# A decoder layer on one core: the prologue of the pair pipeline in another order

## What is computed

```python
def layer(x, c):                                # (32, 64, 256) each
    q, k, v = split(x @ w_project.T)            # 16 heads of 16
    a = softmax(causal(q @ k.T / 4)) @ v
    x = layernorm(x + a @ w_out.T)              # "norm1"
    q, k = rotary(Wq x + bq), rotary(Wk c + bk) # channels on the
    v = Wv c + bv                               #   64 axis, 8 heads of 8
    x = layernorm(x + Wo (softmax(q @ k.T / sqrt(8)) @ v) + bo)
    return layernorm(x + ffn(x))                # two quantised linears
```

## Time and profile before

| | us |
|---|---|
| median of 3 runs | 615.06 (614.21 to 616.49) |
| the profiled execution | 616.69 |
| its span, first to last instruction | 614.5 |
| busy: PE, DVE, ACT, POOL | 477.7, 461.1, 393.7, 301.7 |
| mean granted TensorE clock | 0.814 of full speed |

### The profile page before, as it was taken

One profiled execution on the slowest core, in us unless ns is written; L12 is line 12 of the kernel. 1 busy time (PEld: TensorE's weight loads), 2 busy tenths in 40 slices (PEclk: granted clock), 3 DMA queues, 4 the chain that ended last, 5 costly groups with the idle time before them and its releaser, 6 DMA issues. The chain is left out here.

```text
span 614.5 us, 12481 instructions
## 1 busy us (share of the span) xinstructions
PE 477.7 (78%) x4162; PEld 259.5 (42%) x4162; DVE 461.1 (75%) x954; ACT 393.7 (64%) x729; POOL 301.7 (49%) x430
## 2 busy tenths in 40 slices
PE   5457899999999999999999999798665055544455
PEld 3435445555555455555545544333221033333333
DVE  2544787887987987987987988665467678888885
ACT  1212166767766766766866867777589577777763
POOL 3425546547547447457447445000200577777772
PEclk9666699999999999999999999659669555555555
DMA  5115236333233233223223222100000000000001
GB/s 190 43 22 182 70 88 194 97 83 98 57 83 97 59 84 98 62 77 99 68 70 99 72 58 77 39 2 2 0 1 0 0 0 19 18 17 17 17 17 34
DMA packets 51399, 37.04 MB, mean 60 GB/s; under 512 B 21392, under 2 KB 47376, under 8 KB 51216
## 3 DMA queue, kind: packets, MB, share of 16 engines
q1 hardware_dynamic: 51344, 36.33, 20.9%
HBM read 24.52 MB, written 10.49 MB: 57 GB/s over the span
## 5 line engine op out<-in xcount | busy, mean ns | idle before, releaser
L914 DVE TENSOR_REDUCE MX<-mx_b 128x2 f32<-128x512 f32 x256 | 167.8, 678 | 40.0 <-PE mx_b L541 38.8
L730 ACT ACTIVATE PB<-e_b 128x512 f32<-128x512 f32 x256 | 149.6, 593 | 67.8 <-PE e_b L569 66.9
L541 PE MATMUL mx_b<-KA,QA 48*128 48x256 bf16 x512 | 101.1, 285 | 7.6 <-DVE MX L914 7.5
L569 PE MATMUL e_b<-QA,KA 50*128 50x256 bf16 x512 | 101.4, 282 | 2.3 <-ACT PB L730 2.3
L586 PE MATMUL u_b<-PB,VA 128*32 128x256 f32 x1024 | 86.9, 406 | 3.9 <-ACT PB L730 3.4
L841 POOL TENSOR_TENSOR SP<-SP,srec 128x1024 f32<-128x1024 f32 x16 | 30.4, 1902 | 82.7 <-DVE srec L886 82.7
L541 PEld LDWEIGHTS mx_b<-KA,QA 48*128 48x128 bf16 x512 | 30.2, 95 | 86.2 <-issue 48.6
L1329 PE MATMUL r_b<-att_tab,Q 128*128 128x128 f32 x128 | 31.5, 427 | 37.5 <-ACT Q L1253 37.3
L1321 PE MATMUL z_b<-w2q,Q2T 128*128 128x256 bf16 x128 | 30.2, 417 | 37.0 <-ACT Q2T L1276 31.7
L301 POOL TENSOR_TENSOR rs<-mv,epsc 128x1 f32<-128x1 f32 x32 | 6.1, 192 | 89.0 <-DVE mv L288 58.8
L836 POOL TENSOR_TENSOR KM<-QK,att_tab 128x512 f32<-128x512 f32 x32 | 32.6, 1042 | 30.9 <-ACT QK L684 30.9
(11 more groups left out here) (144 smaller groups left out, 1091.7 us busy)
## 6 DMA issues: line engine op xcount, KB each, us to landing
KA<-parts_k SPq DMA_DIRECT2D x64, 96.0 KB
QA<-parts_q SPq DMA_DIRECT2D x64, 96.0 KB
parts_q<-part_q SPq DMA_DIRECT2D x32, 128.0 KB, 1.9
parts_k<-part_k SPq DMA_DIRECT2D x16, 192.0 KB, 2.1
XT<-in_xT SPq DMA_DIRECT2D x16, 128.0 KB, 2.1
C<-in_ctx SPq DMA_DIRECT2D x16, 128.0 KB, 3.0
X<-in_x SPq DMA_DIRECT2D x16, 128.0 KB, 3.0
out_y<-O SPq DMA_DIRECT2D x16, 128.0 KB, 1.7
```

Of the source, the lines that this page charges most:

```text
L541: m = nc.tensor.matmul(mx_b[n % 2][:, D * k:D * k + D], QA[low:low + K_MAX, 2 * i.ring + b, h, P * u:P * u + P], KA[low:low + K_MAX, 2 * i ...
L569: m = nc.tensor.matmul(e_b[n % 2][:, D * k:D * k + D], KA[low:low + K_EXP, 2 * i.ring + b, h, P * sc:P * sc + P], QA[low:low + K_EXP, 2 * ...
L730: nc.scalar.activation(PB[:, n % 4].rearrange("p e t -> p (e t)"), e_b[n % 2][:, :], ACT.Exp, scale=XC ** -0.5).then_inc(e_sb.sem, 1)
L914: nc.vector.tensor_reduce(MX[:, b, e, 2 * q:2 * q + 2, u], mx_b[n % 2][:, :].rearrange("p (e s) -> p e s", e=2), AXL.X, ALU.max).then_inc( ...
```

## The change

The arithmetic stays. What moves:

- The first loads: wp in two pieces (Q and K, then V, with a semaphore of its own), and XT of pair 0 and the tables issued by ScalarE ahead of its work. A one-element Exp stands first on ScalarE, so that its table load comes there.
- TensorE: QK before V; the waits for tables and fills stand only before their first use; rotary projections and V projections of the prologue write to mx_b and e_b; QK, scores and V of pair 2 come into the prologue, QK of pair 2 ahead of pair 1's transposes.
- Masks of pair 0: half c = 0 on VectorE, c = 1 on GpSimd. KA's fills: ring 0 and 2 on GpSimd, ring 1 on VectorE. `self_norm` of pairs 0 and 1 on VectorE.
- VectorE rotates K of pair 0 behind the subtraction; ScalarE makes norm1 of pair 0 ahead of pair 1's exp, and `v_copy` of pair 1 behind it.
- In the bodies the steps of pair 2 that the prologue now holds are left out (`fresh`).

The diff, cut to its core:

```diff
+        def fresh(pair):
+
+            return real(pair) and pair.v > 2
...
                 elif n == "k":
-                    sp.wait_ge(s_pad, 2 * j.ring + 2)
+                    sp.wait_ge(s_pad[j.ring], 2)
                 sp.wait_ge(stored[n][j.p], NSTORE * (j.uses + 1))
                 dst = {"q": QA, "k": KA}[n]
                 for e in range(2):
...
             p0, p1, p2, p3 = (Pair(0, a) for a in range(4))
-            sp.dma_start(wp[:], wpT.rearrange("(k p) n -> p k n", p=P)).then_inc(ld_wp, 16)
-            load_xT(p0)
-            sp.dma_start(att_tab[:], attn_tables).then_inc(ld_att, 16)
+            wpk = wpT.rearrange("(k p) n -> p k n", p=P)
+            sp.dma_start(wp[:, :, 0:2 * D], wpk[:, :, 0:2 * D]).then_inc(ld_wp, 16)
+            sp.dma_start(wp[:, :, 2 * D:3 * D], wpk[:, :, 2 * D:3 * D]).then_inc(ld_wv, 16)
             load_c(p0)
...
+            def qk_proj(a, bank):
 
                 pe.wait_ge(ld_xT[a.p], 16 * (a.uses + 1))
-                ps = use(g_b[2], qk_sb, a, 1)
+                ps = use(bank, qk_sb, a, 1)
                 for c in range(4):
                     for k in range(2):
                         last = nc.tensor.matmul(ps[:, P * c:P * c + P], wp[:, k, P * c:P * c + P],
                                                 XT[:, a.p, k, :], start=k == 0, stop=k == 1)
                 last.then_inc(qk_ps.sem, 1)
...
-                    wait(pe, km, a, c + 1)
+                    wait(pe, km[c], a, 1)
                     for r in range(2):
                         for b in range(2):
...
-                pe.wait_ge(s_late, 4)
+                pe.wait_ge(s_late, NLATE)
                 nc.tensor.matmul(g_b[g][:, 0:2], ones[:], wsum[:], start=True, stop=True).then_inc(s_wtot, 1)
 
             pe.wait_ge(ld_wp, 16)
-            pe.wait_ge(s_tab, 2)
-            pe.wait_ge(s_init, NINIT)
 
...
-                        qk_proj(a)
+                    if s == 1 and fresh(a):
+                        qk_proj(a, g_b[2])
                     if s == 2 and real(i):
...
             def prologue():
                 p0, p1, p2 = (Pair(0, n) for n in range(3))
-                v_proj(p0)
-                qk_proj(p0)
-                rotary_proj("k", g_b[2], p0)
+                qk_proj(p0, g_b[2])
+                pe.wait_ge(ld_wv, 16)
+                v_proj(p0, mx_b[0])
+                rotary_proj("k", e_b[0], p0)
+                pe.wait_ge(s_tab, 2)
                 scores(p0)
-                qk_proj(p1)
+                qk_proj(p1, g_b[2])
+                pe.wait_ge(s_init, NINIT)
                 transpose_p(p0)
                 self_pv(p0)
-                v_proj(p1)
                 out_proj(p0)
                 scores(p1)
-                rotary_proj("q", g_b[2], p0)
-                rotary_proj("k", g_b[2], p1)
+                v_proj(p1, mx_b[0])
+                rotary_proj("q", mx_b[1], p0)
+                rotary_proj("k", e_b[1], p1)
+                qk_proj(p2, g_b[2])
                 transpose_p(p1)
                 self_pv(p1)
                 out_proj(p1)
-                v_proj(p2)
+                scores(p2)
+                v_proj(p2, e_b[0])
...
                                      scale=winv[:, k:k + 1]).then_inc(s_wround, 1)
 
+            act.dma_start(XT[:, 0], xT[0]).then_inc(ld_xT[0], 16)
+            act.dma_start(att_tab[:], attn_tables).then_inc(ld_att, 16)
             act.wait_ge(s_init, NINIT)
+
+            nc.scalar.activation(warm[:], half[:], ACT.Exp)
 
             def prologue():
                 p0, p1, p2 = (Pair(0, n) for n in range(3))
-                v_copy(p0)
-                qk_copy(p0)
+                qk_copy(p0, g_b[2])
+                v_copy(p0, mx_b[0])
                 self_exp(p0, 1)
                 self_exp(p0, 0)
-                qk_copy(p1)
+                qk_copy(p1, g_b[2])
                 pt_copy(p0)
                 ao_copy(p0)
-                v_copy(p1)
+                norm1(p0)
                 self_exp(p1, 1)
                 self_exp(p1, 0)
-                norm1(p0)
+                v_copy(p1, mx_b[0])
+                qk_copy(p2, g_b[2])
                 pt_copy(p1)
                 ao_copy(p1)
-                v_copy(p2)
+                v_copy(p2, e_b[0])
+                self_exp(p2, 1)
+                self_exp(p2, 0)
 
...
-        def k_mask(pool, a):
-
-            wait(pool, qk_sb, a, 1)
-            for c in range(2):
-                if has(a, 1):
-                    wait(pool, sc_ps, a.plus(-1), 1)
-                nc.gpsimd.tensor_tensor(KM[:, c], QK[:, 2 + c, :].unsqueeze(1).broadcast_to([P, 4, P]),
-                                        kmask.unsqueeze(2).broadcast_to([P, 4, P]), ALU.mult).then_inc(km.sem, 1)
+        def k_mask(eng, ops, a, c, ev):
+
+            wait(eng, qk_sb, a, 1)
+            if has(a, 1):
+                wait(eng, sc_ps, a.plus(-1), 1)
+            ops.tensor_tensor(KM[:, c], QK[:, 2 + c, :].unsqueeze(1).broadcast_to([P, 4, P]),
+                      kmask.unsqueeze(2).broadcast_to([P, 4, P]), ALU.mult).then_inc(ev[c].sem, 1)
+
+        def ones_rows(ops, r):
+            for e in range(2):
+                ops.memset(KA[HALF * e + 32:HALF * e + 64, 2 * r:2 * r + 2].rearrange("p a h t -> p (a h t)"),
+                           1.0).then_inc(s_pad[r], 1)
 
...
             def prologue():
-                p0, p1 = Pair(0, 0), Pair(0, 1)
-                ones_rows(0)
+                p0, p1, p2 = (Pair(0, n) for n in range(3))
+                k_mask(dve, nc.vector, p0, 0, km)
                 row_max(p0, 1)
                 row_max(p0, 0)
-                rotate("k", g_b[2], p0)
                 minus_max(p0, 1)
                 minus_max(p0, 0)
-                ones_rows(1)
+                rotate("k", e_b[0], p0)
                 self_sum(p0)
+                self_norm(dve, nc.vector, p0)
+                ones_rows(nc.vector, 1)
                 norm1_stats(p0)
                 row_max(p1, 1)
                 row_max(p1, 0)
                 minus_max(p1, 1)
                 minus_max(p1, 0)
-                rotate("q", g_b[2], p0)
+                rotate("q", mx_b[1], p0)
                 self_sum(p1)
-                rotate("k", g_b[2], p1)
-                ones_rows(2)
+                self_norm(dve, nc.vector, p1)
+                rotate("k", e_b[1], p1)
                 norm1_stats(p1)
+                row_max(p2, 1)
+                row_max(p2, 0)
+                minus_max(p2, 1)
+                minus_max(p2, 0)
 
...
+            pool.wait_ge(s_ones, 1)
+            pool.wait_ge(s_late, NLATE)
+            pool.wait_ge(s_init, NINIT)
+            ones_rows(nc.gpsimd, 0)
+            pool.wait_ge(s_pad[0], 2)
             pool.wait_ge(ld_att, 16)
-            pool.wait_ge(s_init, NINIT)
 
             def prologue():
-                p0, p1 = Pair(0, 0), Pair(0, 1)
-                k_mask(pool, p0)
+                p0, p1, p2 = (Pair(0, n) for n in range(3))
+                k_mask(pool, nc.gpsimd, p0, 1, km)
                 split_parts(pool, nc.gpsimd, "k", p0)
-                self_norm(pool, nc.gpsimd, p0)
-                k_mask(pool, p1)
+                for c in range(2):
+                    k_mask(pool, nc.gpsimd, p1, c, km)
+                wait(pool, km[1], p1, 1)
+                ones_rows(nc.gpsimd, 2)
+                pool.wait_ge(s_pad[2], 2)
                 rstd(pool, ln1, p0, mv1, rs1)
                 split_parts(pool, nc.gpsimd, "q", p0)
-                self_norm(pool, nc.gpsimd, p1)
+                for c in range(2):
+                    k_mask(pool, nc.gpsimd, p2, c, km)
                 split_parts(pool, nc.gpsimd, "k", p1)
 
```

56 lines of the change are left out of this document (26 added, 30 removed).

## The result

The changed kernel takes **608.5 us** (median of 4 runs, 607.18 to 609.98) against 614.87 for the kernel before, run beside it: a ratio of 0.9893, 95% interval 0.9862 to 0.9925, or 6.4 us. The prediction was 607.1, with a range that takes in 604 and 610, and the measured median lies inside.

The account below looks back on a forecast made before the run. TensorE paces the loop from 79 us; before it a chain of waits bounds the start. First e_b at 70.5 for 78.50, 8.0 us earlier and handed on whole: 615.06 - 8.0 = 607.1 us, range taking in 604 and 610.

Parts of the forecast that it names:

- Start: First loads to the end of pair 0's scores: these end at 12.9 us for 14.80, 1.9 us earlier.
- Pair 0's softmax: Pair 0's scores to transposes: transposes at 19.2 us for 26.20, 7.0 earlier, about 4 from VectorE's two fills.
- VectorE against GpSimd: Rival, chance 0.15: pair 0's normalisation on VectorE waits 0.6 us for GpSimd's split of K; gain 7.4, 607.7 us.
- Pair 1 and the new wait: Pair 1's transposes wait behind QK of pair 2 for its XT: 39.9 us for 48.16, the wait taking back 4.
- First mx_b: First mx_b tile, behind scores and V of pair 2: at 50.6 us for 59.06, 8.5 earlier.
- Body -1: Last piece before the loop: rotary projection waits for norm1 until 53.4 us; first e_b at 70.5 for 78.50, 8.0 earlier.
- the tail: From the V projection of pair 3 to the first e_b in body -1: stays at 6.83 us.
- From there to the end: From the first e_b to the end of the span: the same length as before, 536 us.
- The rival of the high clock: Chance 0.2: the clock rises in body -1 and stays, rotation 0.9 us sooner, tail 1.8 shorter; gain 10.7, 604.4 us.
- The other waits: Rival, chance 0.14: late first load 1.2 us, ScalarE's new order 1, KA's fills on GpSimd 1; gain 5, 610.1 us.
- no effect: Rival, chance 0.05: XT of pair 2 comes another 5 us late, holding pair 1's transposes; gain under 3, 612.5 us.
- slower: Rival, chance 0.02: TensorE waits more in body -1, body 0 runs at the low clock; 619 us with 12 us lost.

Follow-up runs that it names:

- e6: The changed kernel with the first loads as before (wp whole, then XT and the tables, all from SyncE): 609.04 us, ratio 0.9904.
- e2: The changed kernel with V of pair 0 ahead of QK again on TensorE and ScalarE: 609.95 us, ratio 0.9917.
- e3: The changed kernel with VectorE's fill of KA's ring 1 put back ahead of pair 0's sum: 609.83 us over ten runs, ratio 0.9936.
- e4: The changed kernel with the normalisation of pairs 0 and 1 back on GpSimd, behind its split: 609.48 us, ratio 0.989.
- e1: The changed kernel with XT of pair 2 loaded before SyncE waits for pair 1's values: 602.06 us, ratio 0.9776.
- e7: The changed kernel with pair 2's QK, masks, scores and softmax back in body -1, its V still in the prologue: 601.05 us, ratio 0.976.
- e10: The changed kernel with only norm1 of pair 1 moved ahead of pair 2's V copy and exp on ScalarE: 605.32 us, ratio 0.9813.
- e11: The changed kernel itself run and profiled a second time, nothing altered: 606.99 us, ratio 0.9854 to the kernel before.
- e5: The changed kernel with XT of pair 2 loaded early and norm1 of pair 1 ahead of pair 2's V copy and exp: 600.4 us, ratio 0.9731.

## Why the prediction was right, step by step

**Start** (scores end at 12.9): 11.61 + 1.09 = 12.70. The first matmul is at 4.77, where I had 4.9. e6 shows that the loads hardly matter (at most 0.3), and e2 that about 1 us comes from QK ahead of V; the rest isn't taken apart.

**Pair 0's softmax** (transposes at 19.2): 18.82. "About 4 are the two fills" is shown by e3 (4.3). The normalisation was priced as 0.7, the difference of two durations. e4 makes it 2.9, since on GpSimd it would also stand behind K's split; in the kernel before, the two fills had held the sum back until that split was done (20.68). The total held because the split is no cost of the change as made, but the parts don't add up: they were priced against the kernel before, and this one is worth more with the fills gone.

**VectorE against GpSimd** (0.15, 0.6 us later): the mechanism is there, its victim is not the one named. The normalisation took 1.23 us, as elsewhere near 1.18, and L874 of the split 1.65 instead of 0.67, ending 0.53 us behind the end of the normalisation. Twice (17.61 and 32.85) and also with the masks: GpSimd's at 9.36 took 1.45 beside VectorE's, 1.04 alone. By the rule of the Trainium skill (SBUF — State Buffer, "SBUF: two separate sides") the first to start keeps the shared ports for its whole instruction; the rows agree within 0.14 us of the overlap (1.12 us of the normalisation remained, 0.98 us were lost). VectorE began first by 0.11 us, so GpSimd waited. The sum without the 0.6 us was the right one.

**Pair 1 and the new wait** (XT lands at 35.6, QK ends at 39.1, transposes at 39.9, Y at 46.4): 35.89, then 40.45 and 46.91. It is the term that carried the forecast. Without that wait I had the transposes at 35.7, and e1 and e7, which take it away, have them at 33.96 and 33.47: so the wait took back 6.5 to 7 us there, and not the 4 that I gave it. This term was mis-sized; the forecast of where the transposes stand held, because it was made from XT's landing. Most of the 2 us between are the clock again: I had V and the rotary projections of pair 1 at the low level, 2.07 and 2.1 each, and in the change's profile V took 1.13 and each rotary projection 0.9 (Q's from 28.84 to 29.70).

**First mx_b** (50.6): 50.02. **Body -1** (rotary 53.4, rotation 55.5, V of pair 3 63.7, first e_b 70.5): 52.83, 53.97, 63.06, 70.28. norm1 of pair 1 was the wait, as said; by e10's profile it held 1.4 us or more of the path. Behind it the close agreement is partly luck, since three errors cancel. The projection ran fast, so the rotation followed 1.14 us after it and not 2.08, and stood 1.5 earlier than forecast. From the rotation to V of pair 3 it took 9.1 us in both profiles, not 8.2: taking the maxima and subtractions of pair 2 out of body -1 shortened this stretch by 2.0 (from 11.12) and not by 2.9. And the tail took 7.22, not 6.83 (6.29 in e11).

**From there to the end** (536): 537.9 in the first profile, 535.9 in the second. In the first profile it is 1.9 us off, and no step of the change is in it; the prediction took the stretch as fixed, and in that run it isn't.

**The rival of the high clock** (0.2, gain 10.7, 604.4 us) was a clock that rises in body -1 and stays. Its first half came, in both profiles of the change: the rotation 0.9 sooner behind the projection. Its second half came in neither: V of pair 3 took 2.08 and 2.07 us, at the low level (in e3 and e5 it took 1.10). e11's profiled run has the rival's number (604.24) by other ways, and that is chance: against the first profile (609.98) it gains 2.2 us between pair 1's transposes and Y, 0.4 before and 1.1 behind them, and 2.0 behind the first e_b. The clock should have stood in the forecast as its width, in more places than one: the median over nine runs, 607.78, lies between. **The other waits** (610.1), **no effect** (612.5) and **slower** (619) did not come: in the first profile the first e_b came within 0.3 us of the forecast, and the steps ahead of it within 1.6. By the total alone 610.1 can't be excluded, as the ratio's interval reaches from 606.4 to 610.3 us.

## What to carry to other kernels

When steps of a later unit are pulled ahead of a chain's own next step on an in-order engine, look first at the load that they need: here one line of SyncE's order cost some 6 us, nearly as much as the whole change gained. Price a moved instruction against the queue that it would stand in within the changed kernel, not by its duration alone. And before you explain 2 to 4 us by an edit, run one kernel twice: compare starts up to the first place where the clock differs, and behind it only medians of several runs.
